# Four 32-column products with the identity in place of TensorE's transposes of normalised x, q, k and attention a's sums

## The reference, cut to what matters

```
x = x + attn_a(layernorm(x), ...)   # latent attention, 16 heads of 8, causal
x = x + ffn(layernorm(x), ...)      # gated: sigmoid(xr Wr) * (relu(xk Wk)^2 Wv)
x = x + attn_b(layernorm(x), ...)   # 16 heads of 8, q and k scaled to length 1, causal
x = x + ffn(layernorm(x), ...)      # the same weights again
```

## Time and profile before

| | |
|---|---|
| median of three runs | 1035.54 us |
| profiled execution | 1038.37 us |
| its span | 1036.5 us |
| TensorE products (PE) busy | 935.5 us, 90% |
| VectorE (DVE) busy | 846.6 us, 82% |
| ScalarE (ACT) busy | 763.0 us, 74% |
| GpSimd (POOL) busy | 282.6 us, 27% |
| mean granted TensorE clock | 0.975 of full |

### The profile page before, as it was taken

How to read it: one execution, slowest core, us unless ns; L and a number is a source line. 1 busy time by engine, 2 the same in 40 slices (tenths; PEclk the granted TensorE clock), 3 DMA queues, 4 the chain that set the end, 5 groups by cost and what they waited for, 6 DMA issues and landing times.

```text
span 1036.5 us, 43852 instructions
## 1 busy us (share of the span) xinstructions
PE 935.5 (90%) x19167; PEld 522.6 (50%) x19167; DVE 846.6 (82%) x2112; ACT 763.0 (74%) x1042; POOL 282.6 (27%) x264
## 2 busy tenths in 40 slices
PE   3788989989999999999899999999989999999896
PEld 1434545544555555454555555455545555455454
DVE  3978978988798898989799888989898987965733
ACT  2166577768867878887778788887878778898681
POOL 6101223223233132323223132323232232223212
PEclk8689989999999999999999999999999999999999
DMA  5345333374526172643617181633627061505130
GB/s 142 77 112 111 93 105 89 81 154 132 139 66 174 44 204 57 166 105 108 163 58 184 43 224 40 173 94 105 166 79 192 26 202 39 130 5 134 63 74 22
DMA packets 94368, 113.37 MB, mean 109 GB/s; under 512 B 15200, under 2 KB 81888, under 8 KB 94176
## 3 DMA queue, kind: packets, MB, share of 16 engines
q1 hardware_dynamic: 94176, 110.56, 41.3%
HBM read 55.22 MB, written 54.53 MB: 106 GB/s over the span
## 4 chain that ended last, share of the span: by engine, by line
PE 46%; DVE 27%; ACT 14%; issue 6%; DMA 3%; SPq 1%; POOL 1%; POOLq 0%; DVEq 0%; ACTq 0%
PE acc L748 17%; DVE rowmax L1105 11%; PE pool L609 10%; PE pool L731 8%; ACT prob L954 8%; PE pool L660 3%; PE pool L624 3%; DVE ssum L1199 2%; PE pool L676 2%; ACT vals_b L940 2%; ACT vals_a L940 1%; DVE stats L1051 1%; DVE xn L1063 1%; DVE rest_q L1076 1%; DVE step_r L1219 1%
## 5 line engine op out<-in xcount | busy, mean ns | idle before, releaser
L954 ACT ACTIVATE prob<-pool 128x1024 f32<-128x1024 f32 x576 | 567.7, 1034 | 115.7 <-PE pool L676 112.5
L1105 DVE TENSOR_REDUCE rowmax<-pool 128x2 f32<-128x1024 f32 (+7 forms) x480 | 357.0, 791 | 44.7 <-PE pool L676 42.7
L748 PE MATMUL acc<-prob,vals_a 128*32 128x512 f32 (+7 forms) x2048 | 167.3, 418 | 0.0
L748 PE MATMUL acc<-prob,vals_b 128*32 128x512 f32 (+7 forms) x2048 | 162.1, 414 | 3.9 <-issue 2.9
L660 PE MATMUL pool<-stack_ka,stack_qa 48*64 48x512 bf16 (+7 forms) x2048 | 116.9, 297 | 36.4 <-DVE rowmax L1105 11.8
L676 PE MATMUL pool<-mask_t,ident_b 64*64 64x128 bf16 (+1 forms) x2304 | 129.8, 213 | 4.0 <-issue 4.0
L731 PE MATMUL pool<-stack_qa,stack_ka 51*64 51x512 bf16 (+7 forms) x2048 | 110.0, 294 | 16.0 <-DVE rowmax L1105 8.5
L731 PE MATMUL pool<-stack_qb,stack_kb 48*64 48x512 bf16 (+7 forms) x2048 | 109.4, 293 | 7.8 <-DVE rowmax L1105 4.8
L1316 POOL TENSOR_TENSOR rstd<-mv,minus_half 128x4 f32<-128x4 f32 x64 | 65.6, 1025 | 151.5 <-DVE mv L1058 151.5
L660 PEld LDWEIGHTS pool<-stack_ka,stack_qa 48*64 48x64 bf16 x2048 | 43.3, 107 | 99.2 <-issue 51.1
L1328 POOL TENSOR_TENSOR parts_q<-rest_q,parts_q 128x512 bf16<-128x512 f32 x32 | 37.1, 1160 | 190.1 <-DVE parts_q L1079 190.1
(11 more groups left out here) (131 smaller groups left out, 1398.3 us busy)
## 6 DMA issues: line engine op xcount, KB each, us to landing
stack_qa<-scratch_qa SPq DMA_DIRECT2D x64, 192.0 KB, 3.9
stack_ka<-scratch_ka SPq DMA_DIRECT2D x64, 192.0 KB, 4.3
stack_kb<-scratch_kb SPq DMA_DIRECT2D x64, 192.0 KB, 4.5
stack_qb<-scratch_qb SPq DMA_DIRECT2D x64, 192.0 KB, 5.3
scratch_qa<-parts_q SPq DMA_DIRECT2D x16, 384.0 KB, 5.5
scratch_ka<-parts_k SPq DMA_DIRECT2D x16, 384.0 KB, 4.8
scratch_qb<-parts_q SPq DMA_DIRECT2D x16, 384.0 KB, 2.6
scratch_kb<-parts_k SPq DMA_DIRECT2D x16, 384.0 KB, 2.7
```

The lines of the kernel that those rows point to most:

```text
L748: last = eng.matmul(acc[32 * j:32 * j + 32, BLK * blk:T], vals[a][:, blk, GROUP * g + j, :], prob[n % NPROB][:, k, at:at + T - BLK * blk], ...
L954: eng.activation(prob[n % NPROB][:, :, :], place["unit", n][0][:, :, :], ACT.Exp, scale=scale).then_inc(S["exped"], 1)
L1105: last = eng.tensor_reduce(to, of, axis=AX.X, op=ALU.max)
```

## The change

A new function `turned` makes the turn of one 128x128 tile as four products of 32 columns each, with 32 columns of the tile as the stationary operand and the identity (f32, 128x128) as the moving one. The results go to partitions 0 to 31, 32 to 63 and so on of the same place. The three places that turned with `eng.transpose` call it instead. The order of the steps, the waits, the semaphores and the banks stay.

```diff
+            def turned(self, to, of):
+
+                for c in range(0, P, 32):
+                    last = self.eng.matmul(to[c:c + 32], of[:, c:c + 32], ident[:, :], start=True, stop=True)
+                return last
+
@@ layernorm
                 for k in range(NT):
-                    made_ = eng.transpose(ps[:, P * k:P * k + P], xn[n][:, k, :], ident[:, :])
+                    made_ = self.turned(ps[:, P * k:P * k + P], xn[n][:, k, :])
                 made_.then_inc(S["turned" + n], 1)
@@ normalise
                     for k in range(NT):
-                        last = eng.transpose(ps[:, P * k:P * k + P], outT["a"][g][:, P * k:P * k + P], ident[:, :])
+                        last = self.turned(ps[:, P * k:P * k + P], outT["a"][g][:, P * k:P * k + P])
                     last.then_inc(S["outT_turned_a"], 1)
@@ turn_qk
                     for k in range(NT):
-                        last = eng.transpose(ps[:, P * k:P * k + P], qk[:, k, a, :], ident[:, :])
+                        last = self.turned(ps[:, P * k:P * k + P], qk[:, k, a, :])
                     last.then_inc(S[f"projected_{n}b"], 1)
```

## The result

The changed kernel took 1073.67 us (median of four runs, 1071.74 to 1077.06) beside 1034.05 us for the kernel before in the same series: ratio 1.0392, 95% interval 1.0367 to 1.0418, or 39.6 us more. Forecast were 34.8 us more and 1070 us. A later series with six runs gave 1.0433 (1.0401 to 1.0464). The two intervals overlap only a little; 40 to 45 us is what can be said.

What follows compares the result with a forecast made beforehand. TensorE was taken to bound the kernel, VectorE close behind. The chain's turns, 26.7 us, plus 8.1 us from the others made 34.8 us, added to 1035.5 for 1070.3 us; range 1057 to 1084 us.

Steps and rivals of the forecast that it cites:

- The price of a turn: Four-tile turn on TensorE: 0.59 us as transposes; as column products 1.01 us before scores and maxima, 0.87 before weighed sums.
- The sum on TensorE: All 128 turns, in 119 places priced by what follows, add 46.9 us on TensorE.
- what stands ahead costs the same: Work ahead of a turn on TensorE, mostly masks or weighed sums, costs the same with either form; no time added.
- What reaches the end: Of the time added on TensorE by all turns, 34.8 us lengthens the run.
- 40% of the 20.2 us beside the chain: The 55 turns where VectorE or ScalarE holds the chain of waits add 8.1 us to the run.
- the chain's turns bring their 26.7 us: The 73 turns on the chain of waits lengthen the run by their full added time, 26.7 us.
- the cover: TensorE's free time, 5 to 8 us in 100 mid-run, hides part of the 20.2 us of turns beside the chain.
- costs at nothing: Effects taken as free: 32-column weight loads, no added waits, later starts on ScalarE and VectorE, no DMA moved.
- Only the chain's turns: Rival: TensorE's free time hides all 55 turns beside the chain; 1056 to 1063 us, chance 0.18.
- All of it: Rival: TensorE bounds everywhere, so all 46.9 us or more counts; 1082 us, 1085 with shape changes; chance 0.15.
- The clock: Rival: fuller TensorE clock gives back up to 20.5 us; chance of faster 0.02, of a return to within 0.5% 0.03.
- That the change doesn't act: Rival: transposes already run as the same passes as plain products, so nothing moves; within the 0.03 of no change.

Runs made afterwards that it cites:

- the three parts: Kernel before with column products in one place only: layernorms 25.3 us, attention a's sums 14.5 us, q and k of attention b 9.1 us more.
- the whole: The full changed kernel measured again beside the kernel before, on the chip of the follow-up runs: 44.7 us more (41.4 to 47.9).
- the wider forms: Kernel before with each tile turned by one plain 128x128 product or by two of 64 columns: 44.7 and 41.5 us more.

## Why the prediction was right, and what was off

**The price of a turn: right.** The product form was in the trace of before, and its starts carried over to the hundredth: 1.01 and 0.87 us. The factor between transpose and plain product was two.

**The sum on TensorE: right within 4%, in part by luck,** 45.2 us for 46.9. Two misses cancel in it. At the 18 places where TensorE had idled behind the turn it was 0.89 us from start to start before, not 0.59, which takes about 5 us off. At the others the price was a little higher than taken: by the means of the two traces 0.44 us ahead of scores, 0.31 us ahead of weighed sums and more at a few of the lower clock and ahead of warming products, together about 4 us.

The step "what stands ahead costs the same" was wrong in three kinds. Two pairs of rows show one, weighed sums ahead of a layernorm's turn; this is the kernel before, and the changed kernel stands above:

```profile
423.26 0.96 PE L748 MATMUL acc<-prob,vals_b 128*32 128x448 f32 x8
424.15 0.65 PE L624 MATMUL pool<-ident,xn 128*128 128x128 f32 x4
424.74 0.32 PE L748 MATMUL acc<-prob,vals_b 128*32 128x64 f32 x8
424.99 0.41 PE L731 MATMUL pool<-stack_qb,stack_kb 48*64 48x320 bf16 x8
```

The same sums go on after 0.89 us here and after 0.78 us with the column form (432.91 to 433.69), which has their shape; behind values it is 0.52 for 0.57 us. Behind a warming product it is the other way, 0.42 for 0.32 us, as the prediction had feared for the range. And sums behind a turn go on 0.02 us sooner (434.56 to 434.79 against 424.74 to 424.99). Weighted by their numbers, 18 places with sums ahead, 10 with values, 22 with warming products and 51 with sums behind, it comes to about 1 us in the change's favour.

**What reaches the end: the mechanism right, the size too small.** The term that came out too small is "40% of the 20.2 us beside the chain", 8.1 us. If the chain's turns bring their 26.7 us (no run measures that part alone), the measured 39.6 and 44.7 us leave 12.9 and 18.0 us for the other 55, 70 and 86% of the 18.5 and 20.9 us that they took in the two traces.

It wasn't the cover that was misjudged, though. The prediction let TensorE's waits hide 12.1 us, and the named waits shrank by 12.7 and 13.3 us. What it had no term for is TensorE waiting for its instructions, which grew by 4.1 and 8.8 us; it stood in none of the "costs at nothing", though four products take the place of each transpose. In the first trace 47.4 us more busy, less 12.7, plus 4.1 is the 38.8 us by which the span grew.

The cover is used up by the first load: made twice, the turns filled 14.5 us of named waits. The chain reads accordingly. In the changed kernel 112 of the 128 turns are pieces of it (their L615 records on the chain, divided by 32), 73 before, as if the path through VectorE's Newton steps had been overtaken by TensorE's own. A share of less than one held for the first 45 to 56 us of load and not for the next 110.

**The rivals.** Only the chain's turns: out, by the three parts and by the whole. All of it: 44.7 of 47.6 us in the second measurement comes near, but by way of a cover and a cost that it didn't have. The clock: it didn't move (0.975 to 0.978), and the two kernels without warming products show no difference between transposes and products. That the change doesn't act: out by the first row of the timeline.

## What to carry to other kernels

A form of instruction that an added step will have is often in the trace already; take its price from start to start, and once for each kind of neighbour, since a group's length and its mean hide both the overlap and the change of shape. Where the chain changes engine every few microseconds and the busiest engine is at 90%, count work added evenly to that engine at three quarters to all of its length: here 11 to 15 us of waits were there to be filled, once, and whatever came beyond them landed in full. And where one instruction becomes four, count the fetching too: it shows as idle time that no wait explains. In these runs an f32 turn belongs to the transpose: half the time of the product, in any cut.

## What the runs showed that was not expected

Removing 22 us of TensorE's work that nobody reads, the warming products, made the kernel 5.3 us slower and its clock 0.974 instead of 0.980. Moving one slot per batch cost 23.0 us, over half of what 3584 added records and 45 us of TensorE's time cost. And 45 to 48 us on TensorE as 32-column products cost as much time as 52 to 56 us in the wider forms, and more than 49 us of doubled transposes: in the traces TensorE waited longer for its instructions in the first, and was less at the lower clock in the others. Why the clock and these waits fell so isn't shown.
